# Causal attention's first operands made inside offset attention, and work moved across two more stage seams

## The chip, the cores and the metric

One core of one Trainium2 chip runs the whole program as a single launch. The metric is the device time of a run in microseconds (us). The core's engines work side by side, each through its own list of instructions: PE (TensorE, matmuls), ACT (ScalarE), DVE (VectorE), POOL (GpSimd), and SP, which issues the DMAs. They meet only at semaphores, and at the end of a stage, where a new block of instructions begins for all of them.

## The reference, cut to what matters

Two decoder layers over 16 batches of 112 tokens of width 256, with 16 heads of 16:

```
layer 0: future attention -> perceptron gelu(h @ W_ff1) @ W_ff2 -> attention over a memory
         -> mixture of experts
layer 1: offset attention (each weight has a position factor and bias, the result a gate)
         -> causal cross attention: q = h @ Wq + bq, k = ctx @ Wk + bk, v = ctx @ Wv + bv,
            softmax(q k^T / 4 under a causal mask) v, then Wo
         -> quantised perceptron: x and the weights rounded to 8 bit steps; one step for all of x,
            so its largest value over all tokens must be known before the first product
```

Between two stages stands a layer norm of the residual stream. The keys and values of the causal cross attention come from the context, an input, and not from the stage before; its queries come from the normed tokens.

## The kernel before

Tokens are kept feature first (two halves of 128 features, 1792 columns), in four groups of 448 tokens (four batches each). Every product of 128 x 128 weights with 448 float32 columns is one matmul instruction that the profile shows as two records.

`token_attention` (line 1321) serves three stages: "future", "offset" and "causal". Each runs a loop over n = 0 to 17, written out by hand, in which batch n is scored (`scores`, L1472), batch n-1 is turned (transposed, `turn`, L1481) and mixed (`mix`, L1496), and the output of an earlier batch is projected (`output` L1512, `output_of_two` L1521, `output_of_last` L1530). `values(n)` (L1444) makes a batch's values. `pieces(n)` names the key or query products of the next group (`project`, L1438), which are strewn over the iterations: in the offset stage the keys at n % 4 = 1 and 2, in none of n = 13, 14, 15. A piece goes to bank 5, and the second turn of the next iteration writes the same bank, so it waits until the piece has been read. The products of group 0 have no earlier iteration: they stand ahead of the loop, and their readers too (`take_keys` on ACT, L1613, `take_queries` on DVE, L1742). In the causal stage they first wait for the context, which SP loads when the stage begins.

The layer norm of the last group runs beside the first two iterations of the next stage; `Beside` holds its steps: sum (L252), average (PE, L256), centre (DVE, L261), square (ACT, L265), sum of squares (L269), variance (PE, L273), root (ACT, L277 and L279), scale (DVE, L285). The norm of the other groups runs in the same way beside later iterations, group 2's at n = 15 and 16.

`gelu_perceptron` (line 568) makes for each group eight products of 1024 hidden features (L596), two matmuls each, in banks 0 to 3 in turn; ACT applies gelu (L620), after loading its table (L616). `quantised` (line 2502) first turns the rounded weights with 36 bf16 transposes (L2579, L2581), each copied by ACT on its own (L2636, L2638), in three parts between the steps of the last group's norm; DVE then finds the largest token value (L2702), the step is worked out, and the first product is L2595.

In the offset stage `gateT` (128 x 4 x 1792) holds the gates; batch n's part is read at iteration n+1 by `gate` on POOL. SP loads batch n+2's factor rows into a buffer of their own once batch n's are used (L1391).

Of the kernel before, what the change touches and what calls it, by code (L numbers as in the profile page):

```python
# [16 lines left out]
P = 128  # L17
NB, T, D = 16, 112, 256
C = D // P
# [548 lines left out]
def gelu_perceptron(nc, psum, w, hT, accT, yT, beside, next_weights, load_flags, mask_keys):  # L568
# [5 lines left out]
    with Scope(nc, "f0", reuse=True) as s:  # L574
# [11 lines left out]
        def _(pe):  # L586
            for x in (up_ready, hidden_read):
                x.start(pe)
            w.wait(pe)
# [732 lines left out]
def token_attention(nc, kind, stage, psum, const, w, hT, accT, beside, ready, next_weights, ctxT=None, qz_all=None, gateT=None, skewed=None, startup=None, folded=None, big=None, spare=None, room=None, stored=None):  # L1322
# [12 lines left out]
    with Scope(nc, stage, reuse=True) as s:  # L1335
        NM = 2 if offset else 4
        mixT = s.sb("mixT", [P, NM, G])
        if offset:
            gmixT = s.sb("gmixT", [P, 2, G])
        kT = s.sb("kT", [P, 2, 2, G])  # L1340
        v = s.sb("v", [P, NV, H, 32])
        rowmax = s.sb("rowmax", [T, 2, H])
        probs = (big if future else room[1])[0:T, 0:2 * H * T].rearrange("p (u h s) -> p u h s", u=2, h=H) if not causal else s.sb("probs", [T, 2, H, T])
        turned = spare[0:T, 0:4 * HG * T].rearrange("p (i k t) -> p i k t", i=4, k=HG) if offset else s.sb("turned", [T, 4, HG, T])
        NR = 1 if offset else 2
        rden = s.sb("rden", [P, NR, G])
        wt = w.at
        if not offset:
            qz = s.sb("qz", [P, 2, 2, 2, G])
        if causal:  # L1350
            ctx = s.sb("ctx", [P, 2, C, BATCHES_OF, T])
            ctx_loaded = s.loads("ctx_loaded", BATCHES_OF)
# [20 lines left out]
        q_made, q_read = s.counter("q_made", 2), s.counter("q_read", 2)  # L1373
        k_made, k_read = s.counter("k_made", 2), s.counter("k_read", 2)
# [8 lines left out]

        def ctx_load(sp, g):
            for b in range(BATCHES_OF):
                sp.dma_start(ctx[:, g % 2, :, b], ctxT[g * BATCHES_OF + b].rearrange("(c p) s -> p c s", p=P)[:, :, 0:T]).then_inc(ctx_loaded.sem(At(g)), 16)
# [19 lines left out]
        def _(sp):  # L1406
            if startup:
                startup["sp"](sp)
            if causal:
                for g in range(2):  # L1410
                    ctx_load(sp, g)
# [4 lines left out]
            if causal:  # L1416
                for g in range(2, GROUPS):
                    sp.wait_ge(*v_made.after(At((g - 1) * BATCHES_OF - 1)))
                    ctx_load(sp, g)
            if offset:  # L1420
                for n in range(2, NB):
                    sp.wait_ge(*factored.after(At(n - 2), NG - 1))
                    factor_load(sp, n)

        @block.tensor
        def _(pe):
            for x in (q_made, k_made, v_made, scored, tile_turned, mixed, projected) + ((kf_made, vf_made) if future else ()):
# [104 lines left out]

            def read_of(piece):
# [6 lines left out]
            project("k", 0, 0, 6)  # L1540
            project("k", 0, 1, 7)
            if not offset:
# [8 lines left out]
            for n in range(NB + 2):  # L1551
# [3 lines left out]
                if before:  # L1555
# [18 lines left out]
                if ahead < NB:  # L1574
# [5 lines left out]
                    elif causal:  # L1580
                        pe.wait_ge(*q_read.after(At(0), 0))
# [19 lines left out]
        def _(act):  # L1601
            for x in (k_read, exped, copied, mix_copied, logged, inverted) + ((v_read, qm_read, vf_read, fexped) if future else ()):
                x.start(act)
            nc.scalar.preload_act_table_set("natural_log_exp_and_others")

            def take_keys(g, m, bank):
# [5 lines left out]
                else:  # L1612
                    nc.scalar.activation(kT[:, g % 2, m], psum[:, bank, 0:G], ACT.Identity, bias=wt["bk"][:, m:m + 1]).then_inc(k_read.sem, 1)  # L1613

# [1467 lines left out]
```

## Time and profile before

| | us |
|---|---|
| three runs: median (lowest to highest) | 1732.89 (1732.17 to 1736.06) |
| the profiled execution: its own time | 1728.99 |
| its span | 1727.2 |
| PE busy | 1573.6 (91% of the span) |
| DVE, ACT, POOL busy | 892.5, 815.3, 371.0 |

A busy time is a sum over instructions. PE is near full except in a few slices, so what counts is what happens where it is not: at the seams between stages. The stages touched lie at about 60 to 338 us (future attention), 338 to 442 (perceptron), 1327 to 1484 (offset), 1484 to 1659 (causal), and 1659 to the end (quantised perceptron).

### The profile page before, as it was taken

The page shows a single profiled execution, that of the slowest core. Times are in us where ns is not written, and L with a number is a line of the kernel's source. Part 1 is how long each engine was busy: PE and PEld are TensorE (multiplying, and loading weights), DVE is VectorE, ACT ScalarE, POOL GpSimd, SP SyncE. Part 2 cuts the span into 40 slices and gives each one's busy share as a digit, 9 for nine tenths or more (in the row PEclk, how much of TensorE's full clock was granted, in tenths as well). Part 3 has the DMA queues.
Part 4 walks back from the last instruction along what each step waited for, and adds up shares of the span by engine and source line. Part 5 has one row for each costly group of instructions (what it writes and reads, how often), then busy time and mean ns, then how long its engine had stood idle before and what let it go on. Part 6 is the DMA issues. An engine that isn't in the chain of part 4 may idle for free. (4 is left out here: it accounts for less than half of the span.)

```text
span 1727.2 us, 34591 instructions
## 1 busy us (share of the span) xinstructions
PE 1573.6 (91%) x13646; PEld 1027.7 (60%) x13646; DVE 892.5 (52%) x1863; ACT 815.3 (47%) x1616; POOL 371.0 (21%) x337
## 2 busy tenths in 40 slices
PE   8899999899799999999799999999796998799965
PEld 3355555555356666666555999998353666466642
DVE  4566766411555565555242211111464889477758
ACT  4355555533144544454431222222264878456666
POOL 0012121221100000000038100000802777211222
PEclk9999999999999999999799999999998999999998
DMA  7000000100200000000152899996379433000001
GB/s 263 1 1 2 1 1 1 41 15 1 85 19 17 14 19 20 20 11 2 40 185 75 276 325 328 326 326 210 107 185 220 97 77 76 22 12 13 2 1 43
DMA packets 148052, 150.16 MB, mean 87 GB/s; under 512 B 69890, under 2 KB 135107, under 8 KB 147891
## 3 DMA queue, kind: packets, MB, share of 16 engines
q1 hardware_dynamic: 144818, 140.60, 26.5%
q0 software_dynamic: 3072, 7.34, 1.4%
q8 instruction: 109, 1.79, 0.4%
q14 instruction: 53, 0.43, 0.1%
HBM read 120.40 MB, written 27.53 MB: 86 GB/s over the span
## 5 line engine op out<-in xcount | busy, mean ns | idle before, releaser
L2411 DVE TENSOR_TENSOR masked<-masked 128x512 f32<-128x512 f32 x70 | 49.8, 711 | 200.9 <-ACT masked L2313 200.9
L950 DVE CUSTOM_DVE_ANT_0 x_unused<-psum,masked 112x439 f32<-112x439 f32 x256 | 142.0, 611 | 19.0 <-PE psum L773 18.1
L888 ACT ACTIVATE x_probs<-psum,key_mask 125x448 f32<-125x448 f32 x192 | 105.9, 634 | 76.1 <-PE psum L793 76.1
L2254 PEld LDWEIGHTS psum<-mix_xb,mix_up 128*128 128x128 f32 x1120 | 130.6, 192 | 2.1 <-issue 0.4
L2254 PE MATMUL psum<-mix_xb,mix_up 128*128 128x128 f32 x1120 | 130.7, 275 | 0.0
L2264 PE MATMUL psum<-mix_down,masked 128*128 128x256 f32 x560 | 127.0, 380 | 0.1
L1450 PE MATMUL psum<-fold_full,hT 128*112 128x512 f32 x256 | 113.8, 598 | 1.3 <-DVE fold_part L1783 1.3
L2264 PEld LDWEIGHTS psum<-mix_down,masked 128*128 128x128 f32 x560 | 103.6, 190 | 13.2 <-DVE masked L2411 0.4
L773 PE MATMUL psum<-x_kT,x_qz 32*112 32x439 f32 x512 | 86.9, 579 | 3.2 <-DVE x_kT L935 3.2
L2313 ACT ACTIVATE masked<-psum 128x512 f32<-128x512 f32 x70 | 41.8, 597 | 97.1 <-PE psum L2254 97.1
L1024 POOL TENSOR_TENSOR x_mixT<-x_mixT,x_rden 128x448 f32<-128x448 f32 x16 | 18.2, 1138 | 314.7 <-ACT x_rden L894 314.7
L793 PE MATMUL psum<-x_qmax,x_kT 32*125 32x112 f32 (+1 forms) x2048 | 80.3, 283 | 4.6 <-DVE x_qmax L958 3.8
L793 PEld LDWEIGHTS psum<-x_qmax,x_kT 32*125 32x125 f32 (+1 forms) x2048 | 65.1, 176 | 30.0 <-issue 20.9
L1450 PEld LDWEIGHTS psum<-fold_full,hT 128*112 128x112 f32 x256 | 44.1, 177 | 61.4 <-issue 58.9
L807 PEld LDWEIGHTS psum<-x_probs,x_v 125*32 125x32 f32 (+1 forms) x2048 | 47.8, 111 | 46.1 <-issue 25.9
L285 DVE TENSOR_TENSOR hT<-hT,sq 128x896 f32<-128x896 f32 x24 | 26.3, 1094 | 83.2 <-ACT sq L279 83.2
L807 PE MATMUL psum<-x_probs,x_v 125*32 125x112 f32 (+1 forms) x2048 | 65.1, 267 | 4.4 <-ACT x_probs L888 4.1
L1107 POOL DMA_INDIRECT hrow<-slots_y,slot x16 | 15.5, 970 | 248.8 <-POOLq L148 245.3
L1438 PE MATMUL psum<-hT,weights 128*128 128x448 f32 x128 | 56.6, 573 | 7.2 <-issue 4.3
L2319 ACT COPY mix_result<-psum 128x256 f32<-128x256 f32 x35 | 13.0, 372 | 99.1 <-PE psum L2264 99.1
L759 PE MATMUL psum<-weights,x_ctx 128*125 128x256 f32 x192 | 49.5, 394 | 8.3 <-DVE x_kT L935 8.3
L753 PE MATMUL psum<-x_ctx,weights 128*128 128x375 f32 x128 | 53.1, 542 | 3.7 <-DVE x_kT L935 3.2
(335 smaller groups left out, 3323.5 us busy)
## 6 DMA issues: line engine op xcount, KB each, us to landing
mix_up<-in_moe_up SPq DMA_DIRECT2D x35, 1024.0 KB
mix_down<-in_moe_down SPq DMA_DIRECT2D x35, 1024.0 KB
offset_rows<-join_rows SPq DMA_DIRECT2D x16, 784.0 KB, 5.9
hrow<-offset_rows SPq DMA_DIRECT2D x16, 784.0 KB, 5.3
x_ctx<-in_ctxT SPq DMA_DIRECT2D x16, 375.0 KB, 3.1
slots_x<-masked SPq DMA_DIRECT2D x1, 4480.0 KB, 21.3
mix_rows<-slots_x SPq DMA_DIRECT2D x35, 128.0 KB, 3.2
slots_y<-mix_result SPq DMA_DIRECT2D x35, 128.0 KB, 3.4
```

What stands on the lines that cost most here:

```text
L753: mm = nc.tensor.matmul(psum[:, bank, 0:S2], wt["wk"][:, c, m * P:(m + 1) * P], ctx[:, n % 3, c], start=c == 0, stop=c == C - 1)
L759: mm = nc.tensor.matmul(psum[0:CHUNK, 6, k % 2 * D:(k % 2 + 1) * D], ctx[:, n % 3, c, k * CHUNK:(k + 1) * CHUNK], wt["wv"][:, c], start=c ...
L773: nc.tensor.matmul(psum[0:T, bank(*use), 0:KEYS], qz[rows, n // BATCHES_OF % 2, e, m, t:t + T], kT[rows, n % 3, m, e], start=True, stop=Tr ...
L793: mm = nc.tensor.matmul(psum[0:keys_of, bank(*use), k * T:(k + 1) * T], kT[rows, n % 3, m, e, c * CHUNK:c * CHUNK + keys_of], qmax[rows, k ...
L807: mm = nc.tensor.matmul(psum[32 * k:32 * k + 32, 7, g * T:(g + 1) * T], v[0:rows, n % 2, c, HG * g + k, :], probs[0:rows, 4 * (c % 2) + 2 ...
L888: nc.scalar.activation(probs[0:rows, 4 * (c % 2) + r], psum[0:rows, bank("tile", n, 4 * c + r), 0:G].rearrange("p (k t) -> p k t", k=4), A ...
L950: nc.vector.tensor_tensor_reduce(unused[:, at], psum[0:T, at, 0:KEYS], masked[0:T, n * KEYS:(n + 1) * KEYS], -1.0, -3.0 * NEG, ALU.add, AL ...
L1438: mm = nc.tensor.matmul(psum[:, bank, 0:G], wt["w" + name][:, c, m * P:(m + 1) * P], src, start=c == 0, stop=c == C - 1)
L1450: mm = nc.tensor.matmul(psum[0:T, bank, :], hT[:, c, n * T:(n + 1) * T], taps, start=c == 0, stop=c == C - 1)
L2254: mm = nc.tensor.matmul(psum[:, 2 * u + half, m * BLOCK:(m + 1) * BLOCK], e_up[:, w, c, (half * H4 + m) * P:(half * H4 + m + 1) * P], xb[: ...
L2264: mm = nc.tensor.matmul(psum[:, 6 + u, 0:D], e_hidden[:, u, m, :], e_down[:, w, m, :], start=m == 0, stop=m == M8 - 1)
L2411: nc.vector.tensor_tensor(e_hidden[:, u, half * H4:(half + 1) * H4], e_relu[:, half], e_relu[:, half], ALU.mult).then_inc(hidden_ready.sem, 1)
```

## The change

Three moves of work to an earlier place, and what makes room for them.

Perceptron: the first four of group 0's eight hidden products are issued by future attention, two after its iteration 15's pieces and two in iteration 16, ahead of the output of batch 14; each waits until its bank (0 to 3) is free. The gelu table is loaded there too. The perceptron's ACT starts with them, its PE with the fifth.

Causal attention: group 0's context is loaded by SP in the offset stage, after the factor rows of batch 11, into gate memory that is no longer read; the two key products are made at n = 13 and 14, the first query product at n = 15, the second at n = 16. The causal stage starts with `scores(0)`. Its buffers lie in memory of the offset stage. It loads no table, and POOL does the norm's sum before it fills the values' buffer.

Quantised perceptron: the 36 transposes are gathered into six banks, with one copy each. Four are made in the causal stage's iterations 16 and 17, two remain, and DVE's searches for the largest token stand between the norm's steps.

```diff
@@ gelu_perceptron, PE and ACT
-                for m in range(M8):
+                for m in range(UPS_AHEAD if g == 0 else 0, M8):          # UPS_AHEAD = 4
...
-                nc.scalar.preload_act_table(ACT.Gelu)
+                if g:
+                    nc.scalar.preload_act_table(ACT.Gelu)
                 for m in range(M8):
-                    act.wait_ge(*up_ready.after(n, m))
+                    if g == 0 and m < UPS_AHEAD:
+                        act.wait_ge(ups_ahead, m + 1)
+                    else:
+                        act.wait_ge(*up_ready.after(n, m))
@@ before token_attention
+CROSS_CONTEXT_AT = 11
+CROSS_AT = {13: ("k", 0), 14: ("k", 1), 15: ("q", 0)}
@@ token_attention, SP
             if causal:
-                for g in range(2):
-                    ctx_load(sp, g)
+                cross.load(sp, 1)
...
                     factor_load(sp, n)
+                    if n == CROSS_CONTEXT_AT:
+                        sp.wait_ge(*gated.after(At(NB // 2 - 1)))
+                        cross.load(sp, 0)
@@ token_attention, PE
+            def up_ahead(m):
+                if m == 0:
+                    perceptron.wait(pe)
+                    pe.wait_ge(*beside.behind.ready(0))
+                pe.wait_ge(*shifted.after(At(NB - 1), m))
+                for c in range(C):
+                    mm = nc.tensor.matmul(psum[:, m, 0:G], perceptron.at["up"][:, c, m * P:(m + 1) * P], hT[:, c, 0:G], start=c == 0, stop=c == C - 1)
+                mm.then_inc(ups_ahead, 1)
+            def project_cross(name, m, bank):
...
+                for c in range(C):
+                    src = cross.ctx[:, 0, c].rearrange("p b t -> p (b t)") if name == "k" else hT[:, c, 0:G]
+                    mm = nc.tensor.matmul(psum[:, bank, 0:G], cross.w.at["w" + name][:, c, m * P:(m + 1) * P], src, start=c == 0, stop=c == C - 1)
+                mm.then_inc((cross.q_made if name == "q" else cross.k_made).sem, 1)
...
-            project("k", 0, 0, 6)
-            project("k", 0, 1, 7)
-            if not offset:
+            if not causal:
+                project("k", 0, 0, 6)
+                project("k", 0, 1, 7)
+            if future:
...
                     turn(n - 1, 0)
                     for x in pieces(n - 1):
                         pe.wait_ge(*read_of(x))
+                    if offset and n - 1 in CROSS_AT:
+                        name, m = CROSS_AT[n - 1]
+                        pe.wait_ge(*(cross.q_read if name == "q" else cross.k_read).after(At(0), m))
                     turn(n - 1, 1)
+                    if offset and n == NB:
+                        pe.wait_ge(*factored.after(At(NB - 1), 0))
+                        project_cross("q", 1, 0)
...
+                if offset and n in CROSS_AT:
+                    project_cross(*CROSS_AT[n], 5)
+                if future and n in (NB - 1, NB):
+                    for m in range(2):
+                        up_ahead(2 * (n - (NB - 1)) + m)
+                if causal and n >= NB:
+                    for k in range(2):
+                        pe.wait_ge(*shifted.after(At(NB - 1), 2 * (n - NB) + k))
+                        weights.turn(pe, 2 * (n - NB) + k)
                 if last and now and offset:
                     output(n - 2)
                 elif n >= NB:
                     output_of_last(n - 2)
@@ token_attention, ACT
                 if n == NB:
                     copy_mix(n - 1)
+                    if causal:
+                        weights.take(act, 0)
                     take_logs(n - 1)
                     invert(n - 1)
...
+                if n == NB and future:
+                    nc.scalar.preload_act_table(ACT.Gelu)
+                if n == NB and causal:
+                    for k in range(1, TURNS_AHEAD):
+                        weights.take(act, k)
...
+                if offset and n in CROSS_AT and CROSS_AT[n][0] == "k":
+                    take_cross_keys(CROSS_AT[n][1], 5)
                 if offset and before and n < NB:
                     take_logs(n - 1)
@@ token_attention, DVE
                 elif n == NB:
-                    if not offset:
+                    if offset:
+                        take_cross_queries(1, 0)
+                    else:
                         spread_denominators(n - 2)
                     spread_denominators(n - 1)
...
                 if last and now and offset:
                     add_output(n - 2)
                     beside.dve_pair_now(dve, n)
+                    if n in CROSS_AT and CROSS_AT[n][0] == "q":
+                        take_cross_queries(CROSS_AT[n][1], 5)
@@ quantised, PE / ACT / DVE
-            turn(parts[0])
             tail.average(pe, LAST, 7)
-            turn(parts[1])
+            weights.turn(pe, 4)
             tail.variance(pe, LAST, 7)
-            turn(parts[2])
+            pe.wait_ge(*tail.ready(LAST))
+            weights.turn(pe, 5)
...
-            take(parts[0])
             tail.square(act, LAST)
-            take(parts[1])
+            weights.take(act, 4)
             tail.invert_root(act, LAST, 7)
-            take(parts[2])
+            weights.take(act, 5)
...
+            largest_token(0)
             tail.centre(dve, LAST, 7)
+            largest_token(1)
             tail.sum_squares(dve, LAST, nc.vector)
-            for g in range(LAST):
-                largest_token(g)
+            largest_token(2)
             tail.scale(dve, LAST)
```

`take_cross_keys` and `take_cross_queries` are `take_keys` and `take_queries` with other operands: one ACT instruction for a key product, two DVE instructions for a query product. A turn (`weights.turn`) is twelve transposes for k = 0 to 3, eight for 4, four for 5.

## Rows read from the trace of the kernel before

**Rows 1.** The page's first part: busy us (share of the span) xinstructions.

```profile
PE 1573.6 (91%) x13646; PEld 1027.7 (60%) x13646; DVE 892.5 (52%) x1863; ACT 815.3 (47%) x1616; POOL 371.0 (21%) x337
```

**Rows 2.** Timeline, end of future attention: start, length, instructions merged, [idle before <-releaser].

```profile
318.07 1.09 PE L1496 MATMUL psum<-a_turned,a_v 112*32 112x112 f32 x24
321.53 4.98 PE L1521 MATMUL psum<-a_mixT,weights 128*128 128x224 f32 x16 [2.37 <-DVE hT L261]
332.18 5.45 PE L1530 MATMUL psum<-a_mixT,weights 128*128 128x112 f32 x32 [1.29 <-POOL a_mixT L1947]
337.67 0.39 DVE L1841 TENSOR_TENSOR yT<-yT,psum 128x224 f32<-128x224 f32 x1 [0.74 <-PE psum L1530]
338.41 1.28 ACT L616 ACT_TABLE_LOAD   x1 [3.88 <-PEq L148]
338.83 12.27 PE L596 MATMUL psum<-hT,weights 128*128 128x448 f32 x32 [1.20 <-ACTq L74]
```

**Rows 3.** Windows: stretch, us, busy (x) of PE, PEld, DVE, ACT, POOL; granted PE clock.

```profile
322.00:324.00 2.00, 2.00 (x8) 1.86 (x8) 0.77 (x1) 0.46 (x1) 2.00 (x2) 0.61 0.00 0
1488.00:1490.00 2.00, 2.00 (x3) 0.88 (x3) 0.00 (x0) 0.00 (x0) 0.00 (x0) 0.50 0.50 121
```

**Rows 4.** Timeline, end of causal attention: the output of two batches there.

```profile
1645.13 3.29 PE L1521 MATMUL psum<-x_mixT,weights 128*128 128x224 f32 x16 [1.66 <-DVE hT L261]
```

**Rows 5.** Timeline, seam between offset and causal attention.

```profile
1482.93 0.57 DVE L1845 SCALAR_TENSOR_TENSOR xT<-psum,weights,xT 128x112 f32<-128x112 f32 x2 [0.66 <-PE psum L1530]
1487.73 5.97 PE L1438 MATMUL psum<-x_ctx,weights 128*128 128x448 f32 x8 [4.84 <-DMA x_ctx<-in_ctxT]
1495.32 2.82 DVE L1742 TENSOR_SCALAR x_qz<-psum,weights,half 128x448 f32<-128x448 f32 x4 [11.82 <-PE psum L1438]
1498.24 0.94 PE L1466 MATMUL psum<-maskb,identb 112*112 112x448 bf16 x4 [1.53 <-issue]
1500.18 0.63 DVE L1777 TENSOR_REDUCE x_rowmax<-psum 112x4 f32<-112x448 f32 x1 [2.04 <-PE psum L1472]
```

**Rows 6.** Timeline of PE alone, offset attention: scores of batches 6, 7, 8, 13, 14, 15.

```profile
1380.03 1.05 PE L1472 MATMUL psum<-a_kT,qz_all 32*112 32x112 f32 x32
1389.20 1.05 PE L1472 MATMUL psum<-a_kT,qz_all 32*112 32x112 f32 x32
1396.96 1.05 PE L1472 MATMUL psum<-a_kT,qz_all 32*112 32x112 f32 x32
...
1445.54 1.05 PE L1472 MATMUL psum<-a_kT,qz_all 32*112 32x112 f32 x32
1453.44 1.05 PE L1472 MATMUL psum<-a_kT,qz_all 32*112 32x112 f32 x32
1462.19 1.05 PE L1472 MATMUL psum<-a_kT,qz_all 32*112 32x112 f32 x32
```

**Rows 7.** Timeline, offset attention's end; the last is causal attention's second query product read.

```profile
1471.05 0.98 PE L1481 MATMUL psum<-ident,second_result 112*112 112x112 f32 x8 [0.84 <-DVE a_v L1750]
1472.59 1.02 DVE L269 TENSOR_TENSOR sq<-sq 128x448 f32<-128x448 f32 x1
1473.76 0.99 PE L273 MATMUL psum<-sq,averager 128*128 128x448 f32 x2 [1.73 <-DVE sq L269]
1506.28 1.39 DVE L1742 TENSOR_SCALAR x_qz<-psum,weights,half 128x448 f32<-128x448 f32 x2
```

**Rows 8.** Timeline, end of causal attention and head of the quantised perceptron.

```profile
1656.38 2.04 PE L1530 MATMUL psum<-x_mixT,weights 128*128 128x112 f32 x16 [0.44 <-POOL x_mixT L1947]
1659.65 1.82 PE L2579 MATMUL psum<-identb,rounded_weights 128*128 128x128 bf16 x14 [1.23 <-PEq L148]
1659.91 0.63 DVE L252 TENSOR_TENSOR sq<-xT 128x448 f32<-128x448 f32 x1 [0.88 <-PEq L148]
1661.31 0.97 PE L256 MATMUL psum<-sq,averager 128*128 128x448 f32 x2
1667.94 1.08 DVE L285 TENSOR_TENSOR hT<-hT,sq 128x896 f32<-128x896 f32 x1
```

More of the change, by code:

```diff
@@ L588, in _ @@
                 x.start(pe)
+            pe.sem_inc(up_ready.sem, UPS_AHEAD)
             w.wait(pe)
@@ L1423, in _ @@
                     factor_load(sp, n)
+                    if n == CROSS_CONTEXT_AT:
+                        sp.wait_ge(*gated.after(At(NB // 2 - 1)))
+                        cross.load(sp, 0)
         @block.tensor
         def _(pe):
-            for x in (q_made, k_made, v_made, scored, tile_turned, mixed, projected) + ((kf_made, vf_made) if future else ()):
+            for x in (v_made, scored, tile_turned, mixed, projected) + ((q_made, k_made) if not causal else ()) + ((kf_made, vf_made) if future else (cross.q_made, cross.k_made) if offset else ()):
                 x.start(pe)
@@ L1601, in _ @@
         def _(act):
-            for x in (k_read, exped, copied, mix_copied, logged, inverted) + ((v_read, qm_read, vf_read, fexped) if future else ()):
+            for x in (exped, copied, mix_copied, logged, inverted) + ((k_read,) if not causal else ()) + ((v_read, qm_read, vf_read, fexped) if future else (cross.k_read,) if offset else ()):
                 x.start(act)
-            nc.scalar.preload_act_table_set("natural_log_exp_and_others")
+            if not causal:
+                nc.scalar.preload_act_table_set("natural_log_exp_and_others")
             def take_keys(g, m, bank):
@@ L1675, in _ @@
                 act.wait_ge(*stored.after(At(NB - 3)))
-            take_keys(0, 0, 6)
-            take_keys(0, 1, 7)
+            if not causal:
+                take_keys(0, 0, 6)
+                take_keys(0, 1, 7)
             if future:
@@ L1730, in _ @@
         def _(dve):
-            for x in (q_read, maxed, shifted, added) + ((v_read,) if not future else (qk_made, fscored, fmaxed, combined, centred, fsummed, fmixed)) + ((factored, biased_here) if offset else ()) + (spread,):
+            for x in (maxed, shifted, added) + ((q_read,) if not causal else ()) + ((cross.q_read,) if offset else ()) + ((v_read,) if not future else (qk_made, fscored, fmaxed, combined, centred, fsummed, fmixed)) + ((factored, biased_here) if offset else ()) + (spread,):
                 x.start(dve)
@@ L1743, in take_queries, with take_cross_queries @@
                 z.then_inc(q_read.sem, 1)
+            def take_cross_queries(m, bank):
+                if m == 0:
+                    cross.w.wait(dve)
+                    dve.wait_ge(*gated.after(At(NB // 2 - 1)))
+                dve.wait_ge(*cross.q_made.after(At(0), m))
+                for e in range(2):
+                    z = nc.vector.tensor_scalar(cross.qz[:, 0, e, m], psum[:, bank, 0:G], cross.w.at["bq"][:, m:m + 1], const["half"][:, e:e + 1], ALU.add, ALU.mult)
+                z.then_inc(cross.q_read.sem, 1)
             def take_values(n):
@@ L1861, in _ @@
             w.wait(dve)
-            if not offset:
+            if future:
                 take_queries(0, 0, 4)
@@ L1970, in _ @@
                 pool.wait_ge(*stored.after(At(NB - 2)))
-            filled.inc(nc.gpsimd.memset(v[:], 1.0))
+            if causal:
+                beside.pool_sum(pool, 0)
+            filled.inc(nc.gpsimd.memset(v[0:T], 1.0))
             if offset:
@@ L1979, in _ @@
             for n in range(NB + 2):
-                if n == 0:
+                if n == 0 and not causal:
                     beside.pool_sum(pool, n)
@@ L2498, with quantised @@
 POOL_TILES, DVE_TILES = (1, 3), (0, 2, 4, 5)
-def quantised(nc, psum, const, quant, hT, accT, tail, out):
+def quantised(nc, psum, const, quant, weights, hT, accT, tail, out):
     tiles, first = INTER_TILES, INTER_FIRST
-    qb, wscale = quant.rounded, quant.scale
+    wscale = quant.scale
+    (wgT, wuT), wdT = weights.up, weights.down
     LAST = GROUPS - 1
-    turns = [(p, m, c, rows) for p in range(3) for m, rows in tiles for c in range(C)]
-    parts = (range(0, 14), range(14, 26), range(26, len(turns)))
     with Scope(nc, "quant") as s:
-        wgT = s.sb("wgT", [P, C, INTER], BF16)
-        wuT = s.sb("wuT", [P, C, INTER], BF16)
-        wdT = s.sb("wdT", [P, NT_, D], BF16)
         xf = s.sb("xf", [P, C, TOK])
@@ L2628, in _ @@
             h_rounded_last.start(act)
-            def take(some):
-                for k in some:
-                    p, m, c, rows = turns[k]
-                    act.wait_ge(turned.sem, k + 1)
-                    src = psum[:, k % 7, :].bitcast(BF16)
-                    if p < 2:
-                        taken.inc(nc.scalar.copy((wgT, wuT)[p][:, c, first[m]:first[m] + rows], src[:, 0:rows]))
-                    else:
-                        taken.inc(nc.scalar.copy(wdT[0:rows, m, c * P:(c + 1) * P], src[0:rows, 0:P]))
             def scale_tokens(g):
```

115 lines of the change are left out of this document (78 added, 37 removed).

## The prediction

> **What bounds the kernel now.** I read the page's busy shares first: PE is busy 91% of the span [rows 1], so a matmul that only changes place gains nothing unless it lands where PE waits. Then the timeline around the seams, where PE does not work, shows three holes that the change touches.
>
> At the seam between offset and causal attention DVE ends the stage at 1483.50 (1482.93 + 0.57), PE waits 4.84 us for the context, makes the keys in 5.97, then the queries, DVE reads these until 1498.14, and the first score reaches DVE at 1500.18 [rows 5]. That is 16.7 us in which nothing of the attention proper runs.
>
> At the end of future attention PE waits 2.37 us for the norm's centring, then 1.29 for the last normed batches; the perceptron's first product starts at 338.83, 0.77 after DVE's last addition (337.67 + 0.39) [rows 2]. From there PE never waits: 32 records in 12.27 us, one product each 1.53.
>
> The third view is the granted clock. In 322 to 324, behind the wait of 2.37, it is 0.61, and in 1488 to 1490, behind the wait of 4.84, 0.50: the lower level, 1.2 GHz [rows 3]. The price is plain in one shape: the output of two batches takes 4.98 us at 321.53 and 3.29 in causal attention at full clock [rows 2, 4]. So a filled wait can give back more than its length, and a new wait can cost more.
>
> **Perceptron's products ahead.** Removed behind the seam: four products, 4 x 1.53 = 6.1 us of a PE that is never idle. Added before it: the first two, 3.1 us, start where PE stops at 319.16 (318.07 + 1.09) and fill the 2.37: +0.7. The second two fill the 1.29: +1.8 [rows 2]. With the first wait gone I take the output of two at 3.29: -1.7. The two last outputs take 5.45, and one of them at full clock 2.04 [rows 2, 8]: 5.45 - 4.1 gives -1.35. So the stage itself ends 0.55 earlier, in spite of 6.1 us more work. The table load of 1.28 goes to an ACT that waits 3.88 at that point [rows 2]; without that cover it would cost up to 1.28. At the seam PE now waits for the first gelu instead of starting 0.77 behind DVE: estimated +0.35 from the gelu's length less the time PE needed anyway (bounds 0 and 1.3). Part: -6.1 - 0.55 + 0.35 = **-6.3**. If the clock falls all the same, the output keeps its 4.98, the second pair takes 6.1 instead of 3.1 and the last outputs keep 5.45: -6.1 + 0.7 + 1.8 + 3.1 + 0.35, nearly nothing. The other end is -7. I take the full clock, since the trace's fall follows the wait.
>
> **Causal attention's operands.** Behind the seam remain the block's start, 0.77 as at the perceptron, and the mask's products and first scores, 1500.18 - 1498.24 = 1.94 [rows 2, 5]. So 16.7 becomes 2.7: -14.0. POOL's sum comes first now and its fill of the values' buffer second; DVE wants that only after all four score blocks, so it is free. The second group's context is asked for at the same moment as before and used two iterations in: free. If the first matmuls met the lower clock, about 1 us would come back.
>
> What it costs in the offset stage is read from the starts of the scores. The iteration with a piece (batch 6) takes 9.17, the one without (7) 7.76, so a key product on a busy PE costs 1.4. Iteration 13 takes 7.9 and 14 takes 8.75; the latter has waits that a later PE uses up [rows 6]. I take +1.4 and +0.8, so batch 15 is scored 2.2 later (bounds 0.9, both levelled at 9.17, and 3.0, two whole products). The SP queue gets four context loads between the factor rows of 11 and 12, but the rows of 12 wait a further iteration for their buffer, some 9 us [rows 6], so they are not late.
>
> Iteration 15 is where the change adds a wait. The query product goes into bank 5 before the output of batch 13; DVE reads it only behind that output's addition and the norm's sum of squares, and PE's second turn of batch 15 waits for DVE. Behind that turn in PE's list stand the second query product and the norm's variance, and every later turn, mix and output. In numbers: the sum of squares ran from 1472.59 to 1473.61, now 2.2 later, to 1475.8; reading the query product 1.39 more, 1477.2 [rows 7]; the turn 0.5, half of the 0.98 for two; the second product 1.5; so the variance starts at 1479.3 instead of 1473.76: +5.5 in all, 2.2 of it from the keys [rows 7]. Before, the turns at 1471.05 and the variance had waits of 0.84 and 1.73 ahead of them; they would have hidden one product, but not one behind DVE's queue. The end of the stage moves with the variance. Bounds: +2.4 if only PE's own queue counted, +8.5 if the clock falls in the new wait. Part: -14.0 + 5.5 = **-8.5**.
>
> **Quantised weights.** At the head the norm's average stands behind 14 transposes, at 1661.31; the sum it needs ends at 1660.54 (1659.91 + 0.63) [rows 8]. Its centring can then start 0.6 earlier, since DVE does one search first, and the variance no longer waits behind transposes, nor the scale, at 1667.94, behind three searches in a row: I find the scale at 1666.85, -1.1. Bounds -1.5 and -0.4 (the centring's gain less a small wait). In the causal stage a first gathered copy stands ahead of the last logarithm on ACT: about 0.1 late. Twelve transposes stand ahead of the last output, at most 1.82 / 14 x 12 = 1.6 us against 0.44 of wait [rows 8]; but from the eighth on those waited for ACT's copies of single tiles and these do not, so I take +0.1. Bounds 0 and +1.2. Part: **-0.9**. The first product's half clock stays.
>
> **The sum.** -6.3 - 8.5 - 0.9 = -15.7. The profiled execution took 1728.99 (span 1727.2); it becomes 1713.3. The median of the runs shown lies 3.9 higher, and so I put the time at 1732.89 - 15.7 = **1717.2**.
>
> **Rivals.** *The clock falls in the new wait.* Between the first turn of batch 15 (about 1474.4) and DVE's reading (1477.2) PE does nothing for 2.8 us, more than the 2.37 behind which it fell before [rows 2, 3]. Against it: the 1.73 ahead of the variance cost nothing [rows 7]. Then the second query product takes 3.0 and the norm and turns behind it longer: +3.0, 1720.2.
> The Trainium skill, "TensorE: Matmul & The Clock Gate", section "Part 1: The HAM clock gate", says that the throttled state is the default and only activity releases it, so that an idle stretch is paid for by the work behind it. By that rule this rival would hold and the forecast would not; the trace agrees at 322 us (0.61), and no row there shows a wait of this length without a fall.
>
> *The wait on the query product doesn't decide.* If PE reaches the query product and DVE its reading early enough, only 2.4 of the 5.5 remain: 1714.1. For it: DVE had slack in other iterations; against it: the order of its list.
>
> *The perceptron's products run at half clock.* The waits are filled, but the product's start may already be at 1.2 GHz: +4 of the 6.1 possible, 1721.2. Against it: 319.16 lies before the fall.
>
> *Slower than before.* One mechanism: the fall in iteration 15 doesn't end there, and PE stays at 1.2 GHz into causal attention, where it is the bound. Each us at half clock costs half a us; to eat 15.7 it must last 31 us from 1477. The longest stretch of it I find ends within 6 us of matmuls (1487.73 to 1493.70 [rows 5]). At 40 us of it the time would be 1732.89 - 15.7 + 20 = 1737.2.
>
> *The gain is not there.* That the early operands bring nothing would need the causal stage to start on something else late, such as the values' buffer; then 1725.7 (8.5 less gain).
>
> **Chances.** Forecast 0.48, fall in the new wait 0.24, wait that doesn't decide 0.13, half clock in the products 0.08, no gain at the causal seam 0.04, slower 0.03. The range 1712 to 1723.5 takes in the first four, with the bounds of the small terms. 0.2% is 3.5 us, what a measurement here can tell from no change: faster 0.94, same 0.03 (of the case without the gain, whose bounds reach there through the perceptron's), slower 0.03.
>
> **What the profile after would show.** Future attention: PE without a hole at 319, the output of two at 3.3 us, the first gelu right at the seam and no table load there. Offset: scores of 15 some 2.2 later, a wait of PE for DVE (L1742's successor) ahead of the second turn of batch 15, the variance 5.5 later. Causal: from DVE's last addition to its first reduction 2.7 us. Quantised: from the stage's start to the first product 1.1 less. The prediction is wrong if that first reduction is over 4 us behind, if the granted clock is below 1.0 at the offset's end, or if the perceptron's seam brings under 4.

## The result, and the profile after

| us | before | after |
|---|---|---|
| median (lowest to highest, 7 runs each) | 1732.89 (1730.68 to 1736.06) | 1720.16 (1716.57 to 1725.7) |
| ratio, 95% interval | | 0.9924, 0.9909 to 0.9939 |
| span of the profiled execution | 1727.2 | 1714.6 |

The change made the kernel faster by 0.76%. 1717.2 was forecast, 15.7 us less than before; the medians differ by 12.7, the two spans by 12.6. The 12.6 can be divided by the starts of the same instructions in both traces:

| stretch | before | after | difference |
|---|---|---|---|
| start to the scores of batch 15, future attention | 313.78 | 315.52 | +1.7 |
| from there to the perceptron's first down product | 37.90 | 31.40 | -6.5 |
| from there to the offset stage's first scores | 975.46 | 976.28 | +0.8 |
| from there to its scores of batch 13 | 118.40 | 118.44 | 0.0 |
| scores of 13 to scores of 15 | 16.65 | 18.68 | +2.0 |
| scores of 15 to DVE's last addition | 21.31 | 23.89 | +2.6 |
| from there to causal attention's first reduction | 16.68 | 3.39 | -13.3 |
| from there to that stage's last addition | 158.86 | 158.80 | -0.1 |
| from there to the first quantised product | 15.19 | 15.26 | +0.1 |
| the rest | 52.97 | 52.94 | 0.0 |

The first and third rows hold nothing that was changed. Over the twelve traces of this study they wander: the start between 313.6 and 318.8 us; the third takes 975.5 and 976.3 in these two and 963.4 to 968.5 in the ten others.

The page after, its first part. PE's share has stayed, on a shorter span:

```profile
PE 1568.2 (91%) x13646; PEld 1024.7 (60%) x13646; DVE 892.1 (52%) x1863; ACT 812.9 (47%) x1585; POOL 371.5 (22%) x337
```

Timeline of the changed kernel, end of future attention (answers to [rows 2]). The two pairs of products (L1567) stand where PE waited, the output of two (L1548) takes 3.19 instead of 4.98, the two last outputs 3.72 instead of 5.45, and behind the seam ACT starts with four gelus, PE with the fifth product:

```profile
320.83 3.27 PE L1567 MATMUL psum<-hT,weights 128*128 128x448 f32 x8
323.94 3.19 PE L1548 MATMUL psum<-a_mixT,weights 128*128 128x224 f32 x16
331.44 3.27 PE L1567 MATMUL psum<-hT,weights 128*128 128x448 f32 x8
334.55 3.72 PE L1557 MATMUL psum<-a_mixT,weights 128*128 128x112 f32 x32
338.31 0.39 DVE L1930 TENSOR_TENSOR yT<-yT,psum 128x224 f32<-128x224 f32 x1 [0.76 <-PE psum L1557]
339.39 1.85 ACT L628 ACTIVATE f_hidden<-psum 128x448 f32<-128x448 f32 x4 [2.94 <-PEq L74]
340.08 6.25 PE L600 MATMUL psum<-hT,weights 128*128 128x448 f32 x16 [1.81 <-ACT f_hidden L628]
```

The offset stage's end and the seam to causal attention (answers to [rows 5, 7]). PE waits 2.54 us until DVE (L1831) has read the query product, and the variance (L273) is late; behind the last addition (L1934) nothing stands ahead of the mask's products but the start of the block:

```profile
1471.15 1.38 DVE L1831 TENSOR_SCALAR gateT<-psum,weights,half 128x448 f32<-128x448 f32 x2
1472.59 0.60 PE L1508 MATMUL psum<-ident,second_result 112*112 112x112 f32 x4 [2.54 <-DVE gateT L1831]
1474.55 0.92 PE L273 MATMUL psum<-sq,averager 128*128 128x448 f32 x2
1483.64 0.58 DVE L1934 SCALAR_TENSOR_TENSOR xT<-psum,weights,xT 128x112 f32<-128x112 f32 x2 [0.66 <-PE psum L1557]
1485.58 0.93 PE L1493 MATMUL psum<-maskb,identb 112*112 112x448 bf16 x4 [1.98 <-DVEq L74]
1487.60 0.62 DVE L1866 TENSOR_REDUCE x_rowmax<-psum 112x4 f32<-112x448 f32 x1 [3.38 <-PE psum L1499]
```

The quantised head (answers to [rows 8]): average and variance, 0.97 us each before, now take 1.39 and 1.86. First the variance of the kernel before, which [rows 8] leave out, then the changed kernel:

```profile
1665.33 0.97 PE L273 MATMUL psum<-sq,averager 128*128 128x448 f32 x2
```

```profile
1647.96 1.39 PE L256 MATMUL psum<-sq,averager 128*128 128x448 f32 x2 [2.17 <-DVE sq L252]
1652.17 1.86 PE L273 MATMUL psum<-sq,averager 128*128 128x448 f32 x2 [1.97 <-DVE sq L269]
1655.34 1.09 DVE L285 TENSOR_TENSOR hT<-hT,sq 128x896 f32<-128x896 f32 x1 [2.23 <-ACT sq L279]
```

Its windows (stretch, us, busy of PE, PEld, DVE, ACT, POOL, granted clock) say why: from 1648 on the granted clock falls to 0.50, the lower level of 1.2 GHz.

```profile
1646.00:1648.00 2.00, 0.04 (x1) 0.04 (x1) 1.12 (x6) 0.00 (x0) 0.00 (x0) 1.00 0.00 0
1648.00:1650.00 2.00, 2.00 (x10) 1.15 (x10) 1.54 (x2) 0.00 (x0) 0.00 (x0) 0.62 0.00 0
1652.00:1654.00 2.00, 1.83 (x2) 0.50 (x2) 1.11 (x2) 0.35 (x1) 0.00 (x0) 0.50 0.00 0
```

### The profile page after: what moved, and what is told of

It reads as the page before. It is cut to its first block and busy times, and to the rows that moved or that the text cites. A ratio compares the mean times of both kernels' runs of the same rounds, so it can differ in the third digit from the quotient of the medians.

```text
span 1714.6 us, 34568 instructions
## 1 busy us (share of the span) xinstructions
PE 1568.2 (91%) x13646; PEld 1024.7 (60%) x13646; DVE 892.1 (52%) x1863; ACT 812.9 (47%) x1585; POOL 371.5 (22%) x337
## 5 line engine op out<-in xcount | busy, mean ns | idle before, releaser
L1721 ACT COPY masked<-psum 112x448 f32<-112x448 f32 x128 | 63.8, 530 | 60.6 <-PE psum L1508 60.3
L1508 PE MATMUL psum<-ident,second_result 112*112 112x112 f32 x512 | 70.2, 270 | 13.4 <-ACT masked L1721 9.4
L1508 PEld LDWEIGHTS psum<-ident,second_result 112*112 112x112 f32 x512 | 50.9, 136 | 32.4 <-issue 23.6
```

The lines of the kernel that those rows point to most:

```text
L1508: mm = nc.tensor.transpose(psum[0:T, 4 + i % 2, k * T:(k + 1) * T], probs[:, n % 2, HG * i + k], ident[0:T, 0:T])
L1721: nc.scalar.copy(turned[:, i], psum[0:T, 4 + i % 2, 0:G].rearrange("p (k t) -> p k t", k=HG)).then_inc(copied.sem, 1)
```

## The experiments

They ran on other chips: "wait filled" and "keys only" on one where the kernel before takes 1724.1 us, all others on one where it takes 1721.7 to 1722.2. So only ratios are compared across. As every trace wanders in stretches that no kernel here touches, a part is judged by its own stretch of the trace, and the ratio stands beside it. "End" is the time from the scores of batch 15 to DVE's last addition in the offset stage, "seam" from there to causal attention's first reduction, "head" from causal attention's last addition to the first quantised product, "rest" what follows. Every stretch is that of one traced execution, and "full clock" is a granted clock of 1.00.

| kernel | ratio (95%) | end | seam | head | rest |
|---|---|---|---|---|---|
| before | | 21.31 | 16.68 | 15.19 | 52.97 |
| changed, first trace | 0.9924 (0.9909 to 0.9939) | 23.89 | 3.39 | 15.26 | 52.94 |
| changed, second chip | 0.9916 (0.9896 to 0.9936) | 26.94 | 4.94 | 14.88 | 52.96 |
| no products ahead | 0.9960 (0.9944 to 0.9977) | 28.24 | 4.93 | 14.89 | 52.71 |
| no operands ahead | 0.9974 (0.9960 to 0.9988) | 22.79 | 16.54 | 15.74 | 52.84 |
| weights turned in the head | 0.9917 (0.9888 to 0.9946) | 27.73 | 3.81 | 15.23 | 53.2 |
| early read | 0.9896 (0.9868 to 0.9924) | 22.74 | 4.96 | 14.90 | 52.87 |
| matmuls in the head | 0.9910 (0.9896 to 0.9924) | 27.45 | 4.94 | 13.82 | 51.62 |
| transposes in the head | 0.9909 (0.9894 to 0.9924) | 25.31 | 3.39 | 13.82 | 51.63 |
| wait filled | 0.9886 (0.9860 to 0.9913) | 24.41 | 3.36 | 14.89 | 52.94 |
| keys only | 0.9926 (0.9897 to 0.9955) | 21.67 | 9.97 | 14.91 | 53.3 |
| early read, all filled | 0.9879 (0.9862 to 0.9895) | 21.78 | 3.88 | 13.82 | 51.64 |

**No products ahead.**

```diff
-                if future and n in (NB - 1, NB):
-                    for m in range(2):
-                        up_ahead(2 * (n - (NB - 1)) + m)
...
-                for m in range(UPS_AHEAD if g == 0 else 0, M8):
+                for m in range(M8):
```

> The changed kernel with only the perceptron's products put back behind their seam. Theory: the part is worth 6.5 us, of which 6 are the four products and some 1.7 the output of two batches at full clock. So from the scores of batch 15 in future attention to the perceptron's first down product it takes 37.9 us again (31.4 with the products ahead), the output of two takes 5.0 us again behind a wait of 2.4, and the time against the kernel before is about -6 instead of -12.6. Rival, the products only move: then the seam stays within 1 us of 31.4 and the time stays near -12.

The stretch to the first down product took 37.89 us, and 31.36 to 31.40 in the ten traces that have the products ahead, all ten with an output of two of 3.19. The timeline of this kernel shows the wait of 2.37 and the 4.98 of [rows 2] again:

```profile
325.74 4.98 PE L1543 MATMUL psum<-a_mixT,weights 128*128 128x224 f32 x16 [2.37 <-DVE hT L261]
```

The ratio gives -6.9 us (0.9960 of 1721.7) as against -14.5 for the changed kernel on this chip. The part is worth 6.5, of which 1.8 at one output is the clock. Shown.

The surprise was elsewhere: the offset stage's end, whose instructions are those of the changed kernel, took 28.24 instead of 23.89. In this trace the wait is 3.06, and the products and the variance behind it are slow, as is the last output later (3.15 for 2.04). The windows show PE without work, then the fall:

```profile
1471.60 1.00 PE L1503 MATMUL psum<-ident,second_result 112*112 112x112 f32 x4 [3.06 <-DVE gateT L1821]
1472.39 3.22 PE L1573 MATMUL psum<-hT,weights 128*128 128x448 f32 x4
1475.41 1.70 PE L273 MATMUL psum<-sq,averager 128*128 128x448 f32 x2
```

```profile
1469.00:1471.00 2.00, 0.00 (x0) 0.00 (x0) 2.00 (x5) 1.74 (x4) 1.26 (x2) 0.83 0.00 0
1473.00:1475.00 2.00, 2.00 (x4) 1.01 (x3) 0.00 (x0) 0.17 (x1) 0.00 (x0) 0.50 0.04 8
```

**No operands ahead.** The context, the keys and the queries of group 0 at causal attention's start:

```diff
-CROSS_AT = {13: ("k", 0), 14: ("k", 1), 15: ("q", 0)}
+CROSS_AT = {}
...
-            if not causal:
-                project("k", 0, 0, 6)
+            project("k", 0, 0, 6)
```

> The changed kernel with the context, keys and queries of causal attention's group 0 made at that stage's start again. Theory: worth 8.6 us, the difference of 13.3 saved at the seam and 4.7 lost in the offset stage. So from the offset stage's scores of batch 13 to 15 it takes 16.7 us (18.7 with the products), from the scores of 15 to DVE's last addition 21.3 (23.9), from there to causal attention's first reduction 16.7 (3.4). Time against the kernel before about -4. Rival, the 4.7 in the offset stage have another cause, such as the four context loads in SP's queue or the memory that the causal stage borrows: then the 18.7 and 23.9 stay and the time is about 0.

Scores of 13 to 15: 16.65, and seam 16.54: the 2.0 of iterations 13 and 14 are the key products', and the changed memory, which this kernel keeps, costs nothing there. The rival is out. The end took 22.79, not 21.3. Its timeline shows a fall at a wait that was always there, the 1.73 of [rows 7], which left the variance at 0.99 before and leaves it at 1.50 here. By the ratio the part is worth 10 us (-4.5 against -14.5). Timelines of the variance and of the seam:

```profile
1460.53 1.50 PE L273 MATMUL psum<-sq,averager 128*128 128x448 f32 x2 [1.73 <-DVE sq L269]
...
1475.82 5.99 PE L1463 MATMUL psum<-gateT,weights 128*128 128x448 f32 x8 [4.68 <-DMA gateT<-in_ctxT]
```

**Weights turned in the head.**

```diff
-                if causal and n >= NB:
-                    for k in range(2):
-                        pe.wait_ge(*shifted.after(At(NB - 1), 2 * (n - NB) + k))
-                        weights.turn(pe, 2 * (n - NB) + k)
...
+            turn(parts[0])
             tail.average(pe, LAST, 7)
-            weights.turn(pe, 4)
+            turn(parts[1])
             tail.variance(pe, LAST, 7)
-            pe.wait_ge(*tail.ready(LAST))
-            weights.turn(pe, 5)
+            turn(parts[2])
```

> The changed kernel with the 36 transposes and their 36 copies back in the quantised stage's head, the searches in one row again. Theory: the 1.1 us expected of this part were eaten by the clock, which falls in a head without transposes (average and variance then cost 1.3 more). So the granted clock is 1.0 in the head again until the norm's scale, from DVE's last addition to the first product it takes 15.2 us, the same as with the gathered turns (15.3), and the time is the changed kernel's within 0.5. Rival, the gathered turns are worth 1 us and the stage lost it elsewhere: then this kernel's head takes over 16.

Head 15.23 and a ratio of 0.9917, the changed kernel's. The changed kernel's own head took 15.26 and 14.88, so as it stands the third part is worth nothing to 0.3 us. One thing was not as expected: the clock was 1.00 to 1645 but fell before the scale (0.73 in 1645 to 1647). The same instructions, behind the same wait of 1.94 for ACT's copies, kept 1.00 until 1669 in the kernel before.

**Early read.** DVE reads the first query product right behind the values of batch 15.

```diff
                     take_values(n)
+                    if n in CROSS_AT and CROSS_AT[n][0] == "q":
+                        take_cross_queries(CROSS_AT[n][1], 5)
                     if before:
                         spread_denominators(n - 1)
...
-                    if n in CROSS_AT and CROSS_AT[n][0] == "q":
-                        take_cross_queries(CROSS_AT[n][1], 5)
```

> The changed kernel, DVE reading the first query product right behind the values of batch 15, ahead of the spread, the output's addition and the sum of squares. Theory: the wait of 2.5 us ahead of the second turn of batch 15 is DVE's queue; it goes to under 0.5, the variance starts 2.2 earlier, and the stage from the scores of 15 to the last addition takes 21.7 instead of 23.9. Time about 2 less than the changed kernel, -14.8 against the kernel before. Rival, the sum of squares behind it becomes the bound, as it is read first now: then the variance waits for it and only 1 us is left.

The wait is 0.44, and the variance starts 12.12 behind the scores of 15 (1450.00), as against 14.23 in the first trace of the changed kernel: -2.1. The rival is out: the sum of squares ended at 1461.69, 0.4 ahead of the variance. But the end took 22.74, not 21.7, and the seam 4.96, not 3.4. The last output, 2.04 at full clock, took 3.00, behind a wait of 1.87 that was always there, and the mask's products behind the seam 1.71 instead of 0.94: a fall again, one wait later. Timeline of this kernel:

```profile
1460.17 0.59 PE L1508 MATMUL psum<-ident,second_result 112*112 112x112 f32 x4 [0.44 <-DVE gateT L1831]
1462.12 0.92 PE L273 MATMUL psum<-sq,averager 128*128 128x448 f32 x2
1469.14 3.00 PE L1557 MATMUL psum<-a_gmixT,weights 128*128 128x112 f32 x16 [1.87 <-POOL a_gmixT L2040]
1474.11 1.71 PE L1493 MATMUL psum<-maskb,identb 112*112 112x448 bf16 x4 [1.98 <-DVEq L74]
```

**The changed kernel again**, without an edit.

> The changed kernel itself once more, beside the next three. Theory: in the traces so far the same instructions at the offset stage's end took 23.9 us in one execution and 28.2 and 27.7 in two with other parts undone, because the granted clock falls in the 2.5 us wait for the query product in some executions only. So here too the end takes either 23.9 or about 28, and nothing between the stages differs otherwise. Rival, the undone parts caused it: then it takes 23.9 again.

End 26.94, seam 4.94: between the two values expected. The rival is out: the same instructions took 23.89 in one execution and 26.94 in another, and the granted clock in this one is 0.50 behind the wait.

Not all of the 3.05 is the clock: the wait itself is 3.06 here, not 2.54, and that is before the fall. Timelines, two lines of the first trace, then one of this trace:

```profile
1462.65 0.80 DVE L1856 TENSOR_TENSOR second_result<-second_result,weights 112x448 f32<-112x448 f32 x1
1461.82 1.15 POOL L2040 TENSOR_TENSOR a_gmixT<-a_gmixT,a_rden 128x448 f32<-128x448 f32 x1 [1.25 <-ACT a_rden L1716]
...
1451.87 1.32 DVE L1856 TENSOR_TENSOR second_result<-second_result,weights 112x448 f32<-112x448 f32 x1
```

DVE's multiplication starts 2.32 behind the scores in both, but takes 0.80 in one and 1.32 in the other, where POOL's multiplication (L2040) starts 0.5 later. In both it ends 0.48 behind the end of POOL's, and so, within 0.01, in all twelve traces. The two share no tile, so engines hold each other up here without a semaphore, which is more than the opening section allows for. What they share the traces don't show. The long form, and with it a turn 12.8 instead of 12.3 behind the scores, is there in four of the five traces with a fall (not in that of the kernel with transposes, whose wait is 2.55), and in the filled wait below, which has none.

**Matmuls and transposes in the head.** The diff is that of the matmuls; the other kernel has 14, 42, 38 and 48 transposes in these places.

```diff
+            def keep_busy(times):
+                for _ in range(times):
+                    nc.tensor.matmul(psum[:, 5, 0:G], const["identb"][:], quant.rounded[:, 0, 0:G], start=True, stop=True)
+            keep_busy(4)
             tail.average(pe, LAST, 7)
             weights.turn(pe, 4)
+            keep_busy(12)
             tail.variance(pe, LAST, 7)
+            keep_busy(11)
...
             pe.wait_ge(weights.taken, len(TURN_BANKS))
+            keep_busy(14)
```

> The changed kernel with 41 bf16 matmuls of 128x128 by 448 columns into an unused bank on PE in the quantised stage's head: 4 ahead of the norm's average, 12 behind the fifth turn, 11 behind the variance, 14 ahead of the first product. Nothing reads them. Theory (the head's gain was eaten by the clock): they hold it at full speed, average and variance cost 0.95 and 1.0 again instead of 1.39 and 1.86, and the first eight products go at 0.19 us a record: from DVE's last addition to the first product 14.0 us instead of 15.3, and 1 to 2 us more behind it. Rival, the head is bound by DVE and ACT alone: 15.3 stays, or it grows by what the added matmuls delay.

> The same with bf16 transposes of 128x128 in place of the matmuls, 142 of them in the same four places (14, 42, 38, 48), which fill about the same time. Theory (any work on PE holds the clock, as the transposes did in the head of the kernel before): the same 14.0 us. Rival (transposes don't hold it): the clock falls as in the changed kernel, the transposes then take 0.11 each and delay the variance, and the head takes 16 us or more.

Both heads took 13.82 us, both rests 51.6. Timeline of the kernel with transposes: average and variance at 1.02 each, the first products without the half clock (38 records in 7.36, where the first 8 alone took some 3 before):

```profile
1640.01 1.02 PE L256 MATMUL psum<-sq,averager 128*128 128x448 f32 x2
1641.31 2.51 PE L2730 MATMUL psum<-identb,rounded_weights 128*128 128x128 bf16 x42
1643.85 1.02 PE L273 MATMUL psum<-sq,averager 128*128 128x448 f32 x2
1652.27 7.36 PE L2717 MATMUL psum<-quant_xq,weights 128*128 128x448 bf16 x38 [0.36 <-DVE quant_xq L2889]
```

So the head's forecast gain was there and the clock had eaten it: 13.82 is 1.37 less than the kernel before (1.1 was forecast), 1.44 and 1.06 less than the changed kernel's two traces, and 1.3 more is won behind it that the kernel before never had either. Over all traces: in the eight of the changed kernel and its variants that leave the head's waits open the granted clock fell to 0.50 in the head each time, in the three that fill them it stayed at 1.00. Shown. The Trainium skill, "TensorE: Matmul & The Clock Gate", section "Part 4: PE-mode transpose", says that transposes don't count as work for the clock. The runs don't agree: 42 of them take 0.060 us each (2.51 / 42), and the clock stays at 1.00. The measurement decides. The ratios, 0.9910 and 0.9909, can't be told from the changed kernel's 0.9916: 2.7 us in a sum that wanders by more, and in the trace of the kernel with matmuls the offset stage's end took 27.45.

**Wait filled.** The wait for DVE stays as it was, with eleven matmuls in it.

```diff
+                    if offset and n == NB:
+                        pe.wait_ge(*factored.after(At(NB - 1), NG - 1))
+                        for _ in range(11):
+                            nc.tensor.matmul(psum[0:T, 3, 0:G], identb[0:T, 0:T], maskb[:], start=True, stop=True, skip_group_check=True)
```

> The changed kernel, with 11 matmuls that nothing reads (112 rows, 448 columns, bf16, 2.1 us at full clock) on PE ahead of the second turn of batch 15, that is inside its wait of 2.5 us; the wait itself stays as it was. Theory: the wait costs in two parts, DVE's queue (2.1 us, which the early read took away) and, in some executions, a granted clock of half behind it (3 to 4 us more). With the wait filled the second part can't come: no half clock between 1 us before and 6 us behind the second turn, and the variance 14.2 behind the scores of 15, as in the first trace of the changed kernel. The end from the scores of 15 to the last addition takes 23.9, or up to 25 if the clock falls at the later wait for the last batch. Rival, the clock falls for another reason than PE's rest: it is half there in spite of the filled wait, in the three of five cases seen so far.

End 24.41, seam 3.36, all windows from 1458 to 1478 at 1.00; the variance 14.75 behind the scores, where 14.2 was expected. The wait is not shorter: DVE's multiplication took its long form here (1.33), which is the 0.5. Without it the end is the 23.9 of the first trace, so nothing is left for the clock. It is one execution, and one of six with the wait open kept the clock too; taken with the three filled heads, none of which fell, the reading that PE's rest brings the fall is well supported, not proven by this trace alone. Timeline:

```profile
1454.68 2.25 PE L1615 MATMUL psum<-maskb,identb 112*112 112x448 bf16 x11
1457.92 0.60 PE L1508 MATMUL psum<-ident,second_result 112*112 112x112 f32 x4 [1.00 <-DVE gateT L1835]
1459.87 0.92 PE L273 MATMUL psum<-sq,averager 128*128 128x448 f32 x2
```

**Keys only.** `CROSS_AT = {13: ("k", 0), 14: ("k", 1)}`, the query products and their reading at causal attention's start.

> The changed kernel with the context and the keys of group 0 made ahead, the two query products at causal attention's start again. Theory by the terms found: the wait for the query product is gone, so from the scores of 15 to the last addition 21.3 to 22.8 us instead of 23.9 to 28; the seam to the first reduction holds two query products and DVE's reading of them, 3.0 + 2.8 with one product's reading beside, about 8 us at full clock (3.4 in the changed kernel). Together 29.5 to 31, against 27.3 in the changed kernel's best trace and 33.2 in its worst: no clear difference between them. Rival, the queries ahead are worth their full 4.6 us of the seam: then this kernel is 4 us slower than the changed one in every execution.

End 21.67, seam 9.97, together 31.64, where 29.5 to 31 was expected (27.28 and 31.88 in the two traces of the changed kernel), ratio 0.9926. The first expectation holds, that no difference is clear; but the 8 us expected of the seam left out the clock again: it is 0.50 from 1471 to 1475 and 0.62 in the next 2 us, so that the eight records take 5.27 instead of some 3.0:

```profile
1472.42 5.27 PE L1465 MATMUL psum<-hT,weights 128*128 128x448 f32 x8 [1.83 <-PEq L148]
```

So the queries ahead bring 6.6 at the seam (9.97 less 3.39) and take 2.2 at the end (23.89 less 21.67). With the clock's fall behind their wait and at the seam, as in the second trace of the changed kernel, nothing is left of that (31.88 against 31.64).

**Early read, all filled.** The early read, the 41 matmuls in the head, and `keep_warm(bank, times)`, which issues that many matmuls of 112 rows and 448 columns that nothing reads:

```diff
+            if causal:
+                keep_warm(5, 4)
...
+                    if offset and n == NB + 1:
+                        pe.wait_ge(*factored.after(At(NB - 1), NG - 1))
+                        keep_warm(3, 7)
                     output_of_last(n - 2)
```

> The query product read early, as before, the 41 matmuls in the head, and matmuls that nothing reads at two more waits: 7 ahead of the offset stage's last output, 4 ahead of causal attention's first scores (112 rows, 448 columns, bf16). Theory: the clock is full at all three seams, whatever the execution; from the scores of 15 to DVE's last addition 21.7, from there to the first reduction 3.4, head 14.0. With that the time is 3.5 to 6 us under the changed kernel's of the same chip. Rival: the added matmuls delay what follows them by as much as the clock gives.

End 21.78, seam 3.88 (the four matmuls delay the mask's products by 0.5), head 13.82, rest 51.64, and the granted clock 1.00 from the scores of 15 (1453) to 1676, in the quantised stage. The ratio is 0.9879, 0.9862 to 0.9895; the changed kernel's, measured beside it, 0.9916, 0.9896 to 0.9936: 1701.96 us against 1707.37. It is the lowest ratio of this study; the filled wait's 0.9886 and the early read's 0.9896 can't be told from it.

## Why the prediction was right

*Perceptron's part, -6.3 forecast, -6.5 measured.* The terms held within 0.4: the two pairs took 3.27 each, the output of two went from 4.98 to 3.19 (3.29 taken), the last outputs from 5.45 to 3.72 (4.1 taken). Only the seam's entry was short: PE starts 1.38 behind DVE's last addition instead of 0.77, +0.6 where +0.35 was taken. Before, the last outputs ran at a granted clock of 0.67 and 0.50 (332 to 336). So the gain is, roughly, the two waits filled (2.37 + 1.29) and 3.5 of clock (1.8 and 1.7 at the outputs), less 0.6 at the entry. In all ten traces with the products ahead the outputs took 3.19 and 3.72, so the rival of the half clock in the products is out.

*Causal attention's operands, -8.5 forecast, -8.7 measured*, by errors that cancel. Seam: -13.3 for -14.0, as the mask's products start 1.36 behind DVE's last addition (held by DVE's own start of the block, the 1.98 <-DVEq of the row), not 0.77. Iterations 13 and 14: +2.0 for +2.2. The new wait: there as described, 2.54 us, with the variance 2.66 later by iteration 15's own clock (14.23 for 11.57), where 3.3 was taken: the norm's sum of squares came 0.5 sooner, as DVE's multiplication took its short form in this trace. In the filled wait's, with the long form, it is 3.18. The early read shows that the wait is DVE's queue, against the rival that it doesn't decide: that left 2.4 of the 5.5, and with the early read the variance is 2.6 late (2.03 + 0.55).

*The rival of the falling clock had 0.24 and should have had most of the chance.* The first trace escaped it. Of the six traces whose instructions at the offset stage's end are the changed kernel's, one took 23.89; the others 25.31, 26.94, 27.45, 27.73 and 28.24. The windows of all five show 0.50 behind the wait. The end is 1.4 to 4.3 us longer, of which 0.5 in four is DVE's; the clock's own price is 1.4 to 3.8 (3.0 named), and up to 1.55 more at the seam. The prediction's own signs of being wrong, a granted clock below 1.0 at the offset's end and a first reduction over 4 us behind, did not show in the first trace; the first showed in all five others, the second in three (4.93 to 4.94). That the first trace agreed is luck. What the fall does to the median of the first runs a single trace can't say.

*Quantised weights, -0.9 forecast, nothing measured (+0.1 in the head): the term that failed.* The step "I find the scale at 1666.85" took average and variance at the durations of [rows 8]. Those were at full clock with 14 and 12 transposes ahead of them. The part took these away, PE waited 2.17 and 1.97, and the clock fell under them: the average went in part and the variance wholly at half clock. The sentence "The first product's half clock stays" looked at the clock behind the head and not in it. With PE kept busy the gain in the head is 1.4.

*The untouched stretches* took 2.5 us more in the second of the two traces. They were no term and can't be one: they wander by more. Of the spans 15.7 was forecast and 12.6 came: the miss of 3.1 is these 2.5 and the quantised part's 1.0, less 0.4 that the other two parts brought beyond their forecast.

The range held the time. The slower side's mechanism, a half clock that lasts for 31 us, was not seen. The longest stretch from the offset stage's end into causal attention is some 10 us (early read: 0.75, then 0.50 from 1471 to 1479, then 0.69), the longest in any trace is some 17, in the head of the first one (1648 to 1666). The 6 us that the prediction took for the longest was not: in the kernel before the clock is 0.50 from 828 to 840.

## What to carry to other kernels

When work is moved out of a hole, ask what it did for the clock there: putting 6.1 us of products into PE's waits gave 6.5, about half of it clock, and emptying a head cost all of a gain of 1.4. A row's duration holds only with the work that stood ahead of it. Where a new wait on another engine's queue can't be avoided, put the reader first in that queue (2.1 us here), and if PE still rests, matmuls or transposes that nobody reads are worth their room.

## What was not expected of the hardware

The fall of the granted clock is a matter of the execution: the wait for the query product left it at 1.00 in one trace and brought it to 0.50 in five; at its length of 2.54 to 2.55 us it did each once. Behind the waits of 1.73 and 1.87, which the kernel before has and passed at 1.00, it fell in some traces (no operands ahead, early read). One DVE multiplication that runs beside one of POOL ended 0.48 behind POOL's in all twelve traces, and took 0.80 to 1.33 us by when POOL's had started. And bf16 transposes hold it as matmuls do: 13.82 us of head with either.
